# Six weight subtractions move from GpSimd to VectorE, in a routed expert kernel on one core

## The reference, cut to what matters

```python
x = x + low_pass(gelu(x @ W1.T + b1)) @ W2.T + b2        # convolution layer
t = tokens(x)
t = t + attn(layernorm(t))                               # 12 heads of 16, over the heads of one token
t = t + ffn(layernorm(t))

def ffn(x):                                              # 8 experts, hidden width 384, two per token
    probs = softmax(x @ gate_w.T)
    selected_probs, selected_idx = top_k(probs, 2)
    selected_probs = selected_probs / (sum(selected_probs) + 1e-8)
    a, u = x @ gate_bank[e], x @ up_bank[e]
    return sum(selected_probs * ((silu(a) * u) @ down_bank[e]))
```

## Time and profile before

| | us |
|---|---|
| median of 3 runs | 403.89 |
| lowest and highest run | 402.96, 408.67 |
| the profiled execution | 404.54 |
| its span, first to last instruction | 402.6 |
| front block, until the first instruction of the next | 126.5 |
| routing block | 126.5 to 159.2 |
| expert block | 159.2 to the end |

### The profile page before, as it was taken

One profiled execution on the slowest core, in us unless ns is written; L12 is line 12 of the kernel. 1 busy time (PEld: TensorE's weight loads), 2 busy tenths in 40 slices (PEclk: granted clock), 3 DMA queues, 4 the chain that ended last, 5 costly groups with the idle time before them and its releaser, 6 DMA issues.

```text
span 402.6 us, 8457 instructions
## 1 busy us (share of the span) xinstructions
PE 343.7 (85%) x2160; PEld 329.2 (82%) x2161; DVE 268.0 (67%) x731; ACT 220.3 (55%) x538; POOL 268.0 (67%) x276
## 2 busy tenths in 40 slices
PE   6988787887670087999999999999999999999990
PEld 5888676886670087899999999999999999999980
DVE  2588679999798897265666666666656666566650
ACT  2578646886540097245555555555555555555540
POOL 3138665888794001457878887887887887888753
PEclk9999898998555555799999999999999999999996
DMA  6999810444462200224444444444444444444432
GB/s 173 294 355 387 315 70 2 148 128 152 124 184 67 18 1 0 69 50 73 76 75 75 78 70 70 72 76 71 79 74 70 71 77 72 76 76 71 72 39 30
DMA packets 39419, 41.08 MB, mean 102 GB/s; under 512 B 13789, under 2 KB 32448, under 8 KB 39392
## 3 DMA queue, kind: packets, MB, share of 16 engines
q0 software_dynamic: 13824, 16.98, 25.7%
q1 hardware_dynamic: 25568, 23.79, 18.8%
HBM read 25.78 MB, written 14.98 MB: 101 GB/s over the span
## 4 chain that ended last, share of the span: by engine, by line
PE 57%; DMA 1%; issue 0%; POOLq 0%; POOL 0%; ACT 0%; DVE 0%; SPq 0%; ACTq 0%; DVEq 0%
PE moe_ps_y L1154 10%; PE moe_ps_h L1140 6%; PE moe_ps_gt L1129 3%; PE moe_ps_gt L1133 3%; PE moe_ps_gt L1130 3%; PE moe_ps_u L1129 3%; PE moe_ps_gt L1131 3%; PE moe_ps_u L1132 3%; PE moe_ps_gt L1132 3%; PE moe_ps_y L1156 3%; PE moe_ps_u L1131 3%; PE moe_ps_u L1130 3%; PE moe_ps_u L1133 3%; PE moe_ps_x L1120 2%; PE moe_ps_x L1121 2%; PE moe_ps_y L1153 2%
## 5 line engine op out<-in xcount | busy, mean ns | idle before, releaser
L1093 POOL DMA_INDIRECT out<-moe_y,idx_map x71 | 112.9, 1591 | 29.3 <-issue 19.8
L1085 POOL DMA_INDIRECT moe_xt<-rows,idx_map x71 | 69.8, 982 | 56.6 <-POOLq L911 30.2
L1237 ACT ACTIVATE moe_yy<-moe_ps_y,moe_xt 128x384 f32<-128x384 f32 x71 | 41.3, 581 | 71.4 <-PE moe_ps_y L1154 71.4
L1154 PE MATMUL moe_ps_y<-wd,moe_h_hi 128*128 x213 | 70.2, 354 | 0.7 <-DVE moe_h_lo L1300 0.6
L1308 DVE TENSOR_TENSOR moe_y<-moe_yy 128x192 f32<-128x192 f32 x71 | 25.4, 358 | 56.9 <-ACT moe_yy L1237 56.9
L1217 ACT ACTIVATE moe_x_hi<-moe_ps_x 128x256 fp32r<-128x256 f32 x71 | 27.3, 384 | 33.6 <-PE moe_ps_x L1121 33.5
L1300 DVE TENSOR_TENSOR moe_h_lo<-moe_ps_h,moe_h_hi 128x384 fp32r<-128x384 f32 x71 | 39.6, 557 | 2.7 <-ACT moe_h_hi L1229 0.5
L1154 PEld LDWEIGHTS moe_ps_y<-wd,moe_h_hi 128*128 128x128 f32 x213 | 40.2, 189 | 1.3 <-issue 1.3
L1284 DVE TENSOR_TENSOR moe_x_lo<-moe_ps_x,moe_x_hi 128x128 fp32r<-128x128 f32 x71 | 20.7, 292 | 30.6 <-ACT moe_x_hi L1217 30.6
L1294 DVE TENSOR_TENSOR moe_hid<-moe_ps_u,moe_sg 128x384 f32<-128x384 f32 x71 | 38.9, 548 | 0.0
L1156 PE MATMUL moe_ps_y<-wd,moe_h_lo 128*128 x142 | 35.6, 250 | 0.0
(11 more groups left out here) (229 smaller groups left out, 954.5 us busy)
## 6 DMA issues: line engine op xcount, KB each, us to landing
w_lo<-in_wgu SPq DMA_DIRECT2D x8, 768.0 KB, 14.3
xs<-in_x SPq DMA_DIRECT2D x8, 388.0 KB, 7.9
rows<-front_xr SPq DMA_DIRECT2D x8, 384.0 KB, 2.7
out<-xs SPq DMA_DIRECT2D x8, 384.0 KB, 3.5
wd<-in_down SPq DMA_DIRECT2D x8, 288.0 KB, 4.6
xta<-in_xT SPq DMA_DIRECT2D x8, 256.0 KB, 5.1
moe_xt<-rows,idx_map POOLq DMA_INDIRECT x71, 2.8
out<-moe_y,idx_map POOLq DMA_INDIRECT x71, 3.6
```

The source lines that it names most:

```text
L1085: nc.gpsimd.indirect_dma_start(xt[:, slot, :], None, rows.ap(), bass.IndirectOffsetOnAxis(ap=idx_map[:, j, 0:1], axis=0)).then_inc(gathere ...
L1093: nc.gpsimd.indirect_dma_start(out, bass.IndirectOffsetOnAxis(ap=idx_map[:, j, 1:2], axis=0), y[:, j % YR, :], None, compute_op=ALU.add).t ...
L1154: ins = nc.tensor.matmul(both, hi, halves, start=(k == 0), stop=(k == 2))
L1237: nc.scalar.activation(yy[:, s].rearrange("p h c -> p (h c)"), ps_y[:, s, 0:2 * C], ACT.Copy, scale=xt[:, slot, bass.ds(GC + e, 1)]).then_ ...
```

## The change

GpSimd's six subtractions for experts 5 to 7 are taken out of the front block. VectorE does them instead as its first work in the expert block, ahead of its wait for the index copy. A new semaphore, ready, is raised by the last of the six, and TensorE waits for it after its 4 keep_busy matmuls, ahead of reading the first expert number. The three subtractions that VectorE did ahead of the early choice stay there.

```diff
@@ -680,9 +680,6 @@
                     if QUADS - 1 - READY <= n < QUADS - 1:
                         split_down(n - (QUADS - 1 - READY))
                 deviation(last)
-                for e in range(READY, EXPERTS):
-                    split(e)
-                    split_down(e)
 
             @block.vector
             def _(dve):
@@ -1070,6 +1067,7 @@
         clear = a.sem("clear")
         xt_done, gate_done, up_done, ht_done, y_mm = (a.sem(n) for n in ("xt_done", "gate_done", "up_done", "ht_done", "y_mm"))
         x_hi_done, x_lo_done, x_lob_done = a.sem("x_hi_done"), a.sem("x_lo_done"), a.sem("x_lob_done")
+        ready = a.sem("ready")
         silu_done, hid_done, weighed = a.sem("silu_done"), a.sem("hid_done"), a.sem("weighed")
         h_hi_done, h_lo_done, y_done = a.sem("h_hi_done"), a.sem("h_lo_done"), a.sem("y_done")
         N = TILES_MAX
@@ -1189,6 +1187,7 @@
                 keep_busy(11)
                 turn_x(0, 0)
                 keep_busy(4)
+                pe.wait_ge(ready, 1)
                 for r in range(2):
                     e = expert(0, r)
                     gate_product(0, r, e)
@@ -1270,6 +1269,10 @@
                 for c in (x_lo_done, x_lob_done, hid_done, h_lo_done, y_done):
                     dve.sem_inc(c, RING)
 
+                for e in range(READY, EXPERTS):
+                    for low, high in ((w_lo[:, e, 0], wa_hi[:, e]), (wd[:, e, 1], wd[:, e, 0])):
+                        ins = nc.vector.tensor_tensor(low, low.bitcast(F32), high.bitcast(F32), ALU.subtract)
+                ins.then_inc(ready, 1)
                 dve.wait_ge(top_in, 16)
                 nc.vector.tensor_tensor(above[:, 1:TILES_MAX], top[:, 1:TILES_MAX, 1],
                                         idx_map[0:1, 0:TILES_MAX - 1, 1], ALU.is_ge).then_inc(above_done, 1)
```

## The result

| | before | with the change |
|---|---|---|
| median of 20 runs, us | 406.16 | 401.59 |
| lowest and highest run | 402.96, 409.76 | 399.11, 406.41 |
| span of the profiled execution | 402.6 | 399.7 |

The ratio is **0.9898**, with a 95% interval of 0.9876 to 0.9920: about 4.1 us faster, with 3.2 to 5.0 us inside the interval. Two more timings of the same kernel gave 0.9880 (0.9845 to 0.9916) and 0.9869 (0.9805 to 0.9933). The forecast's ratio, 0.988, lies in all three intervals. (Runs more than 1.5% above the fastest of the same kernel are left out of the ratios, not of the medians.)

A forecast was written before the change was run, and what follows sets the result against it. VectorE's early choice, lengthened by GpSimd's subtractions, was taken to end the front block; TensorE bounds the expert block. The sum -4.93 + 0.1 = -4.8 us gave a median of 399.1 us, ratio 0.988, range 397.8 to 402.0.

The forecast's parts named there:

- VectorE's early choice ends the front block, GpSimd makes it long: Front block: VectorE ends last, at 126.24 us; six rows take 1.05 to 1.85 us instead of 0.36 during GpSimd's subtractions.
- 4.93 us saved, ScalarE next: Front block's end: moves from VectorE's 126.24 to ScalarE's 121.31 us, saving 4.93 us; bounds 0 and 4.93.
- The six cost 4.67 us: Expert block's head: six VectorE subtractions take 4.67 us, mostly covered; head cost 0 to 0.4 us, taken as 0.1.
- A gather waits for at most one subtraction, its 1.05 us of cover holds: Expert block's head: GpSimd's gather may wait at most some 0.9 us for VectorE, within 1.05 us of cover; cost nothing.
- Gathers do not hold VectorE: Expert block's head: VectorE's subtractions are not slowed beside gathers, as L1308 rows stay at 357 to 360 ns.
- the first rival: Expert block's head: the first three gathers each block a subtraction, gate product about 2.6 us late, 401.7 us; chance 0.14.
- The clock rival: Expert block's head: gathers' 2.6 us stall plus 3.1 us from TensorE restarting at half clock, 404.7 us; chance 0.04.
- The clock that rises earlier: Expert block's head: TensorE's clock rises earlier, x_low gains 0.13 and first matmuls some 0.3 us, 398.6 us; chance 0.08.
- a sign of being wrong: Expert block's head: the prediction called itself wrong if TensorE idles ahead of the first gate product; no size given.
- the gathers' rival: Expert block's head: gathers block VectorE's subtractions for their whole length, 2.6 us lost, 401.7 us; chance 0.14.
- half a gain: Front block: only half the saving from the early choice comes, 401.5 us; chance 0.05.
- cases in which nothing is saved: Two cases near 404 us: early choice's rows stay long (0.04), or stall plus TensorE's clock eats the gain (0.04).

## Why the prediction was right, and where not

- **VectorE's early choice ends the front block, GpSimd makes it long:** shown. The six rows fell to 0.36 each, and came back to 1.05 to 1.85 us in the kernel that has GpSimd's six again (stretch two 18.31 us).
- **4.93 us saved, ScalarE next:** measured 4.95 in two profiles, in which SyncE still waited 0.6 and 0.8 us. In the first it was 4.71, since SyncE's write ended 0.2 us after ScalarE's copy. The prediction had SyncE done at 120.8, only 0.5 us ahead of ScalarE, and did not carry it on as a third engine that could set the end.
- **The six cost 4.67 us:** 161.39 - 156.77 = 4.62. Start assumed 0.29 us after the block's first row, measured 0.51. Together x_low is 0.01 us later; cost 0 of the assumed 0.1.
- **A gather waits for at most one subtraction, its 1.05 us of cover holds:** the first gather took 1.64 us, 0.66 over the median, the next 1.16 and 1.20. TensorE's first turn still followed its 11 matmuls at once, 4.48 us after the block's first row as before. The cover was 0.85 us rather than 1.05: the turn's own row starts at 163.65 in the kernel before, not at the 163.85 at which the matmuls end.
- **Gathers do not hold VectorE:** the subtractions have the same durations beside them and without; the first rival falls. That VectorE is held up for a whole GpSimd instruction is seen at GpSimd's two-input subtractions and not at its gathers.
- **The clock rival:** its mechanism exists, and begins where it was put, at a stall of TensorE at the head; twelve subtractions showed it. Its price was 1.55 us against 3.1: the prediction had 6.2 us of work at half clock and took half of all of it as lost; measured, the clock was back after some 5 us, and 1.55 us is less than half of them.
- **The clock that rises earlier:** it did in all three profiles, to different degrees (the 4 keep_busy matmuls took 1.31, 1.50 and 0.94 us instead of 1.63). The first gate product came at 6.38, 6.35 and 6.32 us against 6.38, so it gained 0.06 at most and not the rival's 0.4. This is also why TensorE was idle ahead of it, by 0.31 and 0.85 us in the first and third, which the prediction had called a sign of being wrong; it was none, for TensorE was idle there without the six too.
- **The time, 399.1:** the measured median is 401.59. The ratio was right; the base was not. I hung the number on a median of three runs, 403.89, and 20 runs of the same kernel gave 406.16. This base is the term that was mis-sized, 2.3 us of the 2.5; the other 0.2 is the saving, 4.57 us between the medians against 4.8. That 401.59 still lies inside 397.8 to 402.0 is in part luck: the upper end had been set for the gathers' rival and for half a gain, and neither came.
- **The chances:** the step that failed is the resolution. The prediction took it that a measurement tells "about 2% from no change", for which it had no row, and so gave 0.96 to within 2%. Its own sum was 1.2%, and half the width of the interval is 0.22% in the first timing and 0.2 to 0.6% in all of them, so that a gain of 1.0% stands clear of no change. By the sum, most of the chance belonged to a gain that can be measured; only 0.08 was on cases in which nothing is saved.

What stays open: the 0.7 us between 4.8 and the first ratio's 4.1 lies inside its interval, and no stretch of the profiles holds it. Why the first 108 us of the front vary by 5 us is not shown either.

## What to carry to other kernels

When the last engine of a block does many small instructions, compare equal shapes inside its own timeline: those that take longer only while GpSimd computes show a gain that moving GpSimd's work gives back, though GpSimd itself is not on the path. Bound the gain by every engine that ends next, the writes of SyncE too, and when something is started earlier, ask for the input that will then be late. Work put into a wait at a phase's head was free here up to its cover and dearer than its length beyond it (6.1 us for 4.6), as TensorE's clock fell in the same wait. Take the base of a forecast in microseconds from more than three runs, or forecast the ratio alone.

## What the runs showed of the hardware that was not expected

- GpSimd held up a VectorE instruction with two SBUF inputs until its own instruction ended if that was a TENSOR_TENSOR with two inputs (0.7 to 1.5 us more on 0.36), by 0.4 to 0.6 us, and only one that began together with it, if it was a TENSOR_SCALAR with one, and not measurably if it was a memset or a gather.
- A gather beside VectorE's subtractions took 1.16 to 1.64 us, against 0.95 to 1.06 in the kernel without them.
- A VectorE TENSOR_SCALAR on 24 values per partition took 1.82 us beside memsets, against 0.18; beside GpSimd's multiplications the same one took 0.18.
- TensorE's granted clock rose to full, was lost during a stall of 4.84 us and was back some 5 us after work resumed at 167.1.
